# Router logits collected per tile inside the self-attention loop, and only the dense tiles turned behind it

## The reference

```python
logits = xt @ Wg                      # xt: layer norm of x, (4096, 128); Wg: (128, 8)
probs = softmax(logits)
_, top_idx = top_k(probs.T, 512)      # every expert takes its 512 best tokens
tok2exp = argmax over the experts that took the token, or over all if none did
out = sum_e gate_e * (gelu(xt @ W1[e]) @ W2[e])
```

## Time and profile before

| | before |
|---|---|
| median of 3 runs | 813.57 us (811.36 to 815.04) |
| the profiled execution | 814.61 us, span 812.5 us |
| PE busy | 698.5 us (86%) |
| DVE busy | 630.8 us (78%) |
| ACT busy | 510.2 us (63%) |
| POOL busy | 380.6 us (47%) |
| mean granted clock of PE | 0.935 |

### The profile page before, as it was taken

The page is one execution under the profiler, slowest core; times in us unless marked ns, Lnnn a source line. Parts: engine busy times, 40 slices in busy tenths (PEclk is TensorE's granted clock), DMA queues, the critical chain, the costliest instruction groups (busy, mean ns, idle before and its releaser), DMA issues.

```text
span 812.5 us, 27814 instructions
## 1 busy us (share of the span) xinstructions
PE 698.5 (86%) x9162; PEld 562.0 (69%) x9162; DVE 630.8 (78%) x1500; ACT 510.2 (63%) x1629; POOL 380.6 (47%) x380
## 2 busy tenths in 40 slices
PE   3572999999999999999999856799999689999565
PEld 1241767677777777777777645688888578889465
DVE  5462989899999999999999858589988656759721
ACT  1451777777777777787778624688888434545242
POOL 1250364456544654553544249477777320006365
PEclk9976999999999999999999979799999759999788
DMA  7558344444444444443440030000000000006980
GB/s 165 96 97 225 81 86 81 96 92 90 92 91 95 87 96 85 97 83 81 92 83 13 2 105 1 2 3 3 0 0 3 2 1 1 1 1 196 290 253 23
DMA packets 195179, 60.75 MB, mean 75 GB/s; under 512 B 147557, under 2 KB 193513, under 8 KB 195123
## 3 DMA queue, kind: packets, MB, share of 16 engines
q1 hardware_dynamic: 192000, 55.65, 30.7%
q0 software_dynamic: 1824, 3.96, 1.4%
q10 hardware_dynamic: 1298, 0.40, 0.2%
HBM read 51.58 MB, written 8.83 MB: 74 GB/s over the span
## 4 chain that ended last, share of the span: by engine, by line
PE 50%; SPq 17%; DVE 10%; issue 9%; ACT 7%; POOL 3%; ACTq 1%; DMA 1%; DVEq 0%; POOLq 0%
PE energy L485 22%; PE bank L485 15%; PE bank L488 13%; SPq L516 9%; ACT PR L644 6%; DVE STAT L1465 2%; SPq L522 2%; DVE X L1738 2%; SPq L566 1%; SPq L564 1%; POOL SX L907 1%; SPq L561 1%; POOL TQ L899 1%; ACTq L644 1%; SPq L539 1%
## 5 line engine op out<-in xcount | busy, mean ns | idle before, releaser
L644 ACT ACTIVATE PR<-energy,STAT 128x256 f32<-128x256 f32 x512 | 234.4, 482 | 107.5 <-DVE STAT L1465 107.5
L1465 DVE TENSOR_REDUCE STAT<-energy 128x512 f32 (+1 forms) x256 | 164.3, 685 | 27.2 <-PE energy L485 26.9
L488 PE MATMUL bank<-ident,PR 128*128 128x128 f32 x1024 | 152.5, 283 | 21.6 <-DVE PT L1482 16.8
L1482 DVE COPY PT<-bank 128x512 f32<-128x512 f32 x256 | 161.9, 672 | 1.3 <-PE bank L488 1.3
L488 PEld LDWEIGHTS bank<-ident,PR 128*128 128x128 f32 x1024 | 109.7, 142 | 52.6 <-issue 40.3
L833 POOL TENSOR_TENSOR QB<-QT,headmask 128x512 f32<-128x512 f32 x32 | 33.3, 1039 | 196.1 <-DMA MK<-in_mask_BxSxS_ik 122.1
L644 ACT ACTIVATION_READ_ACCUMULATOR PR<-energy,STAT (+1 forms) x512 | 110.1, 215 | 0.0
L840 POOL TENSOR_SCALAR MZ<-MK 128x512 bf16<-128x512 int32 x64 | 94.3, 1491 | 0.0
L485 PEld LDWEIGHTS bank<-wv_s,CT 128*128 128x128 f32 x512 | 68.7, 196 | 32.3 <-issue 31.8
L485 PE MATMUL bank<-CT,wk_s 128*128 128x512 f32 x128 | 68.5, 618 | 7.2 <-DVE CT L1489 7.2
L485 PE MATMUL bank<-PT,VT 128*32 128x128 f32 x2048 | 70.1, 278 | 0.2 <-DVE PT L1482 0.2
(11 more groups left out here) (268 smaller groups left out, 1340.6 us busy)
## 6 DMA issues: line engine op xcount, KB each, us to landing
CX<-in_ctx SPq DMA_DIRECT2D x512, 32.0 KB, 2.2
MK<-in_mask_BxSxS_ik SPq DMA_DIRECT2D x128, 128.0 KB
rows_in<-fill SPq DMA_DIRECT2D x1, 3483.0 KB, 19.0
X<-in_x SPq DMA_DIRECT2D x4, 512.0 KB, 7.7
VLT<-v_last SPq DMA_DIRECT2D x4, 512.0 KB, 8.2
QT<-in_L_ffn_W SPq DMA_DIRECT2D x16, 128.0 KB
OT<-in_L_ffn_W SPq DMA_DIRECT2D x16, 128.0 KB
PAY<-rows_in SPq DMA_DIRECT2D x2, 903.0 KB, 8.2
```

The lines of the kernel that those rows point to most:

```text
L488: return nc.tensor.transpose(o, i, ident[0:n, 0:n])
L644: nc.scalar.activation(PR[:, b, g, :], EB[:, g, e * KEYS:(e + 1) * KEYS], ACT.Exp, bias=STAT[:, bass.ds(t, 1), b, 1, g:g + 1].rearrange("p ...
L1465: V.tensor_reduce(STAT[:, bass.ds(t, 1), b:b + 2, 1, g:g + 1].rearrange("p a b g -> p (a b g)"), EB[:, g, :].rearrange("p (e k) -> p e k", ...
L1482: V.tensor_copy(PT[:, k % 2, e, 2 * half:2 * half + 2, :].rearrange("p g k -> p (g k)"), psum[1 if e else 7]).then_inc(ev_t, 1)
```

## The change

The logits are taken apart. With x2 = x1 + O @ w_o, mean m2 and r2 = 1/std2 of x2, and xn1 = (x1 - m1) / std1, the tile that self-attention has turned anyway:

logits = r2 * (std1 * (xn1 @ Wg) + O @ (w_o @ Wg) + (m1 - m2) * colsum(Wg)).

So inside self-attention PE multiplies two stationary tiles that it has there, xt and SO, by 8 columns each: xt with wg_s, and SO with wlog = sw_o @ wg_s, which is made once in the course of cross-attention. The results of all tiles stay in one PSUM bank (2 x 256 columns). Behind the loop DVE puts them together over 128x256. The statistics of the second norm get tiles of their own (mv2, std2, rstd2), since std and mean of the first are still needed. The normalisation of X moves to GpSimd: tiles 0 to 11, turned by PE in three groups (`turn_dense`) into banks 4 and 5 and copied by ACT behind the exponential; then the 20 others straight into PAY, with no transpose. router_step(0) stands between the second and the third group.

```diff
@@ ACT, in the loop of cross-attention's end
             for u in range(NT // 4 + 1):
+                if u == 4:
+                    act.wait_ge(lg_tr, 1)
+                    nc.scalar.activation(SO[:, 0, :], psum[4][:, 0:P], ACT.Copy).then_inc(lg_wo, 1)
+                if u == 6:
+                    act.wait_ge(lg_pe, 1)
+                    nc.scalar.activation(wlog[:, :], psum[5][:, 0:2 * E], ACT.Copy).then_inc(lg_w, 1)
@@ ACT, behind self-attention
             act.wait_ge(n2_std, 1)
-            nc.scalar.activation(std[:, :], std[:, :], ACT.Sqrt).then_inc(n2_rstd, 1)
-            def evac_router(u, h):
...
-            for u in range(NT // 4):
-                evac_router(u, u % 2)
+            nc.scalar.activation(std2[:, :], std2[:, :], ACT.Sqrt).then_inc(n2_rstd, 1)
+            nc.scalar.activation(warm[:, :], warm[:, :], ACT.Exp)
             act.wait_ge(t_act, 1)
             nc.scalar.activation(PRB[:, :, :], PRB[:, :, :], ACT.Exp).then_inc(t_exp, 1)
+            for u in range(LATE):
+                act.wait_ge(r_tr, u + 1)
+                wait_reuse(act, r_xl, u - 1)
+                nc.scalar.activation(xg[:, u % 2, :], psum[4 + u % 2], ACT.Copy).then_inc(r_xt, 1)
+                nc.scalar.activation(XH[:, u * 512:(u + 1) * 512], psum[4 + u % 2], ACT.Copy).then_inc(r_xh, 1)
@@ GpSimd, behind self-attention
-            for u in range(LATE):
-                input_rest(u, u % 2)
-            pool.wait_ge(a_x2, NT)
+            pool.wait_ge(r_inv, 1)
+            for u in range(LATE + 1):
+                if u < LATE:
+                    wait_reuse(pool, r_tr, u - 1)
+                    for j in range(4):
+                        normalised(xn[:, u % 2, j, :], 4 * u + j).then_inc(r_xn, 1)
+                if u:
+                    input_rest(u - 1, (u - 1) % 2)
+            for t in range(DENSE, NT):
+                normalised(PAY[:, t - DENSE, 0:P], t).then_inc(r_pn, 1)
             nc.gpsimd.tensor_copy(PAY[:, :, P:2 * P], X[:, DENSE:NT, :]).then_inc(pay_x, 1)
@@ PE, in the loop of cross-attention's end
+                if u == 3:
+                    pe.wait_ge(ld_s, N_S)
+                    pe.wait_ge(m_inv, 1)
+                    tr(psum[4][:, 0:P], sw_o[:, :]).then_inc(lg_tr, 1)
+                if u == 5:
+                    pe.wait_ge(lg_wo, 1)
+                    mm(psum[5][:, 0:E], SO[:, 0, :], wg_s[:, :])
+                    mm(psum[5][:, E:2 * E], ones_s, wg_s[:, :]).then_inc(lg_pe, 1)
@@ PE, in project(t, j) and project_out(t, j)
+                mm(psum[1][:, bass.ds(NT * E + t * E, E)], xt[:, j, :], wg_s[:, :])
+                mm(psum[1][:, bass.ds(t * E, E)], SO[:, j, :], wlog[:, 0:E])
                 mm(psum[7][:, P:2 * P], SO[:, j, :], sw_o[:, :]).then_inc(a_wo, 1)
@@ PE, behind self-attention
-            for u in range(NT // 4 + 1):
-                if u < NT // 4:
-                    turn_router(u, u % 2)
-                if u:
-                    logits(u - 1, (u - 1) % 2)
+            def turn_dense(u):
+                if u == 0:
+                    pe.wait_ge(a_sx, NT)
+                wait_reuse(pe, r_xt, u - 1)
+                wait_reuse(pe, r_xh, u - 1)
+                for j in range(4):
+                    pe.wait_ge(r_xn, 4 * u + (j + 1))
+                    last = tr(psum[4 + u % 2][:, j * P:(j + 1) * P], xn[:, u % 2, j, :])
+                last.then_inc(r_tr, 1)
...
+            def first_of_group(i):
+                pe.wait_ge(r_xl, i + 1)
+                if i == 0:
+                    pe.wait_ge(ld_ffn, 32)
+                    pe.wait_ge(w1_l, 1)
+                    pe.wait_ge(r_lg, 1)
...
+            turn_dense(0)
+            turn_dense(1)
             router_step(0)
+            turn_dense(2)
@@ DVE, behind self-attention
-            moments_to_rstd(n2_std, n2_rstd)
-            for u in range(NT // 4 + 2):
-                if u < NT // 4:
-                    norm_router(u, u % 2)
-                if u >= 2:
-                    keep_logits(u - 2, u % 2)
+            moments_to_rstd(n2_std, n2_rstd, mv=mv2, std=std2, split=True)
+            added, own = (psum[1][:, k * NT * E:(k + 1) * NT * E].rearrange("p (i e) -> p i e", e=E) for k in range(2))
+            dve.wait_ge(a_wo, NT)
+            link(V.tensor_tensor(rmx[:, :], mv[:, :, 0], mv2[:, :, 0], ALU.subtract))
+            link(V.tensor_tensor(PRB[:, :, :], own, over_experts(std[:, :]), ALU.mult))
+            V.tensor_tensor(PRB[:, :, :], PRB[:, :, :], added, ALU.add).then_inc(r_lg, 1)
+            dve.wait_ge(r_lg, 1)
+            link(V.tensor_tensor(KEY[:, :, :], over_experts(rmx[:, :]),
+                                 wlog[:, E:2 * E].rearrange("p (a e) -> p a e", a=1).broadcast_to([P, NT, E]), ALU.mult))
+            link(V.tensor_tensor(PRB[:, :, :], PRB[:, :, :], KEY[:, :, :], ALU.add))
+            dve.wait_ge(n2_rstd, 1)
+            V.reciprocal(rstd2[:, :], std2[:, :]).then_inc(r_inv, 1)
+            dve.wait_ge(r_inv, 1)
+            link(V.tensor_tensor(PRB[:, :, :], PRB[:, :, :], over_experts(rstd2[:, :]), ALU.mult))
```

More of the change, by code:

```diff
@@ L141, in perceiver_block @@
         shift = sb("shift", [P, NT])
+        mv2 = sb("mv2", [P, NT, 2])
+        std2 = sb("std2", [P, NT])
+        rstd2 = sb("rstd2", [P, NT])
+        wlog = sb("wlog", [P, 2 * 8])
         STAT = sb("STAT", [P, NT, BT, 2, NG])
@@ L404, in perceiver_block @@
         w1_l = sem("w1_l")
+        r_inv = sem("r_inv")
+        r_pn = sem("r_pn")
         r_lg = sem("r_lg")
-        r_cp = sem("r_cp")
+        lg_tr = sem("lg_tr")
+        lg_wo = sem("lg_wo")
+        lg_pe = sem("lg_pe")
+        lg_w = sem("lg_w")
         t_act = sem("t_act")
@@ L954, in input_rest, with normalised @@
                                         XH[:, bass.ds(u * 512, 512)], ALU.subtract).then_inc(r_xl, 1)
-            for u in range(LATE):
-                input_rest(u, u % 2)
-            pool.wait_ge(a_x2, NT)
+            def normalised(dst, t):
+                return nc.gpsimd.tensor_scalar(dst, X[:, t, :], mv2[:, t:t + 1, 0], rstd2[:, t:t + 1],
+                                               ALU.subtract, ALU.mult)
+            pool.wait_ge(r_inv, 1)
[8 more added lines that the diff above has]
+                normalised(PAY[:, t - DENSE, 0:P], t).then_inc(r_pn, 1)
             nc.gpsimd.tensor_copy(PAY[:, :, P:2 * P], X[:, DENSE:NT, :]).then_inc(pay_x, 1)
@@ L964, in _ @@
             pool.wait_ge(filled, 16)
-            pool.wait_ge(r_xn, NT)
+            pool.wait_ge(r_pn, SORTED)
             pool.wait_ge(s_gate, 1)
@@ L1158, in _ @@
                     out_project(u - 1, (u - 1) % 2)
+            pe.wait_ge(lg_w, 1)
             pe.wait_ge(wqk_ok, 1)
@@ L1221, in _ @@
                           (1, self_values), (4, turn_probs)], NT, 4, 6)
-            pe.wait_ge(a_x2, NT)
-            def turn_router(u, h):
+            def turn_dense(u):
+                if u == 0:
+                    pe.wait_ge(a_sx, NT)
                 wait_reuse(pe, r_xt, u - 1)
-                wait_reuse(pe, r_xh, min(u - 1, LATE))
+                wait_reuse(pe, r_xh, u - 1)
                 for j in range(4):
                     pe.wait_ge(r_xn, 4 * u + (j + 1))
-                    t = 4 * u + j
-                    last = tr(psum[h][:, j * P:(j + 1) * P], PAY[:, t - DENSE, 0:P] if t >= DENSE else xn[:, h, j, :])
+                    last = tr(psum[4 + u % 2][:, j * P:(j + 1) * P], xn[:, u % 2, j, :])
                 last.then_inc(r_tr, 1)
[L1235 to L1240, removed]
-            for u in range(NT // 4 + 1):
-                if u < NT // 4:
-                    turn_router(u, u % 2)
-                if u:
-                    logits(u - 1, (u - 1) % 2)
[L1249 to L1252, removed]
+            def first_of_group(i):
[4 more added lines that the diff above has]
+                    pe.wait_ge(r_lg, 1)
             def hidden(i, e, between):
                 u = i * E + e
+                if e == 0:
+                    first_of_group(i)
                 for j in range(FC):
@@ L1269, in expand @@
                 pe.wait_ge(f_g, u * FC + FC)
-                if not (isinstance(u, int) and u < 2):
+                if u < 2:
+                    pe.wait_ge(r_xh, LATE)
+                else:
                     pe.wait_ge(f_keep, u - 1)
@@ L1380, in link, with moments_to_rstd @@
                 dve.wait_ge(dve_c, chain[0])
-            def moments_to_rstd(st_sem, rs_sem, count=1, tiles=slice(0, NT), done=None):
+            def moments_to_rstd(st_sem, rs_sem, count=1, tiles=slice(0, NT), done=None, mv=mv, std=std, split=False):
                 me, mo = stats[:, tiles, 1], stats[:, tiles, 4]
@@ L1398, in moments_to_rstd @@
                 V.scalar_tensor_tensor(std[:, tiles], mv[:, tiles, 1], 0.25, std[:, tiles], ALU.mult, ALU.add).then_inc(st_sem, 1)
+                if split:
+                    return
                 dve.wait_ge(rs_sem, count)
```

16 lines of the change are left out of this document (removed).

## The result

| | before | after |
|---|---|---|
| median of 10 runs | 813.08 us (811.36 to 815.04) | 820.02 us (816.16 to 821.51) |
| the profiled execution | 814.61, span 812.5 | 821.51, span 819.5 |
| mean granted clock of PE | 0.935 | 0.932 |

The changed kernel is slower by 0.84%: ratio 1.0084, 95% interval 1.0070 to 1.0099. I had forecast 812.5 and a range of 806 to 819.5.

The account below looks back on a forecast made before the run. Bound: the chain of self-attention loop, router-logit stretch, dense experts with bisection, then sorted rows. Stretch -13.0, loop +7.7 and +1.0, port +3.0, cross-attention +0.2 sum to -1.1 us on 813.57: 812.5 us, range 806 to 819.5.

Parts of the forecast that it names:

- the loop's: Self-attention loop: two added products per tile cost +7.7 us, their register addresses +1.0 us.
- GpSimd's price for a normalisation: Between loop and experts: one 128x128 f32 normalisation on GpSimd takes 0.60 us, bounds 0.455 and 0.80.
- the stretch: From last residual to first expert matmul: transposes, logit products and DVE normalisations go, so experts start 13.0 us earlier.
- The port: During the experts: GpSimd work delays DVE's `trial` and `thr` in four bisection rounds, 2.6 us, plus 0.4 for the copy: +3.0.
- What bounds the loop: Self-attention loop: a chain through the engines every two tiles sets 7.40 us, while PE alone needs 3.40 a tile.
- PE's own step: Self-attention loop: PE's work per tile grows from 3.40 by 0.44 to 3.84 us; counting only this, 4.5 us in all.
- the two-tile loop: Self-attention: chain over PE, ACT, DVE and GpSimd once per two tiles grows from 7.40 to 7.84 us, 3.92 a tile.
- Cross-attention: One transpose, two products and two copies added where GpSimd sets the pace: +0.2 us (0 to 1).
- rival C: Slower: added weight loads in self-attention fall wholly on the path, 14.4 us plus 1.8 for registers; 820.0 us, chance 0.12.
- C's point of decision: Self-attention loop: the added cost per tile from which this slower case decides, 0.28 us.
- B's loop: Faster: self-attention grows only by PE's own step, 4.5 us, registers and port cost nothing; 805.3 us, chance 0.30.
- D's condition: Slower: a GpSimd normalisation costs 1.0 us, delaying experts and meeting seven bisection rounds (+6.3); 820.6 us, chance 0.10.

Follow-up runs that it names:

- experiments 6: Kernel before the change, plus both products per tile at fixed addresses, placed at the end of PE's step behind turn_probs: ratio 1.0053 to before, loop 136.3 us.
- experiment 8: Changed kernel with both products moved to the end of PE's step, behind turn_probs: ratio 0.9982 to before, median 810.72 us.
- the second execution: The unaltered changed kernel profiled again later, beside other runs: ratio 1.0081 to before, loop 142.8 us.
- experiment 7: Changed kernel with the PAY copy on ACT, dense tiles normalised on DVE and router steps two `between` calls later: ratio 0.9951 to before, median 808.67 us.
- experiment 3: Changed kernel without the two products per tile in the self-attention loop: ratio 0.9911 to before, median 805.22 us.

## Why the prediction was wrong

**The steps that failed.** The parts that I had added up to -1.1 us came to +3.7 in the profiled execution (+1.8 in the second), and the medians moved by +6.9. The term that was off most is the loop's: 7.7 and 1.0 us for the two products, where it grew by 11.6 (10.9). Next is GpSimd's price for a normalisation: 0.60 us, where it took 0.79 to 0.83, so that the stretch shrank by 11.8 and not 13.0. The port's 3.0 us was near in size but came from another instruction than the one that I priced. And the first stage, for which I had no term, took longer in every kernel with the change. Each in turn:

**What bounds the loop: right.** PE's own step of 3.40 + 0.44 and the two-tile loop of 7.40 + 0.44 were both confirmed, the first by the 3.84 of experiments 6 and 8, the second by the 3.95 a tile of the written-out steps (3.92 forecast) and by what happens when the products leave it. One reading behind it was luck: I took the step from 581.62 to 585.02 for one without a wait, but the QD ahead of it ended at 584.95 (583.91 + 1.04), 0.07 us before the scores, the distance of the steps that wait. That PE's own step is 3.40 is borne out only by 3.84 - 0.44. What I didn't do is draw the conclusion that stood in my own sum: it had 4.5 us for the products if only PE's own step counts, and the loop with the products at the end grew by 4.4.

**Size of the loop's term: too small.** Forecast +8.7, measured +11.6 (10.9 the second time). Over 26 tiles in the steady part 4.02 - 3.70 = 0.32 a tile, 8.3 us, where I had 0.22 and 1.0 for the registers, 6.7. From the start of the scores to the start of turn_probs, and from there to the scores two steps on, it is 3.01 + 4.38 in most steps of before, 3.23 + 4.38 with one product, 3.53 + 4.38 with two at fixed addresses, and 3.65 + 4.43 with two at register addresses. So the two products put 0.52 us into the two-tile loop, where I had 0.44 (and where the same two add 0.44 to PE's own step), and the register addresses another 0.17. The rest, 3.3 us, is filling and draining, for which 2.0 stood. About 1 us of it is the distance between the first two scores alone: 4.10 in after and 3.19 in the second execution, against 2.96 before; among the kernels with both products it was 3.2 to 4.5, so that part varies by about a microsecond.

**The stretch: right in kind, 1.2 us short.** -11.8 for -13.0. The term that was mis-sized is the normalisation on GpSimd. The groups of after:

```profile
L968 POOL TENSOR_SCALAR PAY<-X,mv,rstd 128x128 f32<-128x128 f32 x20 | 15.6, 794 | 0.0
L968 POOL TENSOR_SCALAR xn<-X,mv,rstd 128x128 f32<-128x128 f32 x12 | 9.9, 833 | 9.0 <-DVE rstd L1673 9.0
```

It takes 0.79 alone, where I took 0.60 near the row of the same operation and size that writes bf16; my upper bound was 0.80. Twelve make 12 x 0.19 = 2.3 us more. The meetings with DVE, for which I added 1.3, made it 0.83 instead of 0.79, 0.5 in all. The Trainium skill (GPSIMD Engine Reference, section 3.1), by which I had estimated a shorter instruction and a start a microsecond earlier, erred on the same side; the measurement decides.

**The port: right in sum (+3.0, measured +4.0 and 2.8), wrong in its cause.** I gave 2.6 us to four rounds of `trial` and `thr` beside normalisations and 0.4 to the copy. In after the operations beside normalisations have a mean of 0.22, 0.18 and 0.18 us for `trial`, `trial_next` and `thr`, against 0.16 each once GpSimd is silent: together 0.1 us a round, not 0.75; the longest was 0.28, and the rounds were 2.7 us long, not 3.3. The copy did nearly all of it, in a single instruction: with the copy on ACT the stage was back at 62.6. That could have been read from the trace of before. There the same copy lay beside DVE's normalisations: four took 1.83 us without it, and 3.67 with it.

```profile
649.85 1.83 DVE L1406 TENSOR_SCALAR PAY<-X,mv,rstd 128x128 f32<-128x128 f32 x4
...
652.30 3.67 DVE L1406 TENSOR_SCALAR PAY<-X,mv,rstd 128x128 f32<-128x128 f32 x4
653.06 2.32 POOL L960 COPY PAY<-X 128x2560 f32<-128x2560 f32 x1
```

I had looked for long GpSimd instructions where they stood and not asked which of them the change moves beside the bisection. The Trainium skill (SBUF — State Buffer, "Who interferes with whom") says of such a meeting that the blocked engine waits for the whole instruction of the other; the copy and the subtractions of experiment 7 agree, the normalisations, 0.79 us each, don't. In after the rows don't show the copy first either: `thr` begins at 690.04, 0.26 us ahead of it and during the last normalisation, and still ends with the copy. What decides there is open. PE's idle time can cost more than itself: in after and in experiment 8 PE's weight loads stood still for 2.55 and 2.54 us, its clock then fell to 0.50, and the stage took 66.5 us. In the second execution and in experiment 3 they stood for 2.00 and 1.90 us, the clock stayed at 1.00, and the stage took 65.3. Of the 1.2 us between the two pairs some 0.6 is the longer idle time itself; the other 0.6 goes with the clock, by this estimate, and not the whole of what a stall costs beyond its length.

**Cross-attention: nothing** (34.4 against 34.5), as forecast within 0.2.

**What stays open.** The stages that I looked at sum up to +3.7 us in one profiled execution and +1.8 in the other, the medians differ by 6.9. By the profiled executions the rest lies in the first and the last stage. Profiled executions of kernels with the change had a first stage of 475.4 to 478.8 (seven, mean 477.1), those without 471.8 to 476.7 (five, mean 474.1). The granted clock of PE between 40 and 80 us was anything from 0.71 to 0.78 with the change and from 0.71 to 0.79 without, so a part may be chance. A part isn't likely to be: the longest wait of the first stage is DVE's for a tile of the context, with PE idle behind it, here in before and in after:

```profile
76.53 0.71 DVE L1489 STREAM_TRANSPOSE CT<-CX 128x512 f32<-128x512 f32 x1 [16.74 <-DMA CX<-in_ctx]
```

```profile
79.57 0.71 DVE L1517 STREAM_TRANSPOSE CT<-CX 128x512 f32<-128x512 f32 x1 [18.68 <-DMA CX<-in_ctx]
```

It was 16.7 to 17.3 us in the five profiled executions without the change (mean 16.9) and 18.0 to 18.7 in the seven with it (mean 18.2). So the changed kernel has 1.3 us of its own there, in a place whose code it didn't touch. Why, and what makes up the other 1.7 us between the means, no run settles.

**The rivals.** The measured median is the number of rival C, by chance: C had 16.2 us for the loop, which took 11.6, and the difference was made up by other terms. C's point of decision, 0.28 us a tile, was passed (11.6 / 32 = 0.36). Its mechanism was only half true: not every added weight load falls on the path, but a loop of two tiles in which both stand. B's loop (4.5) is what experiments 6 and 8 show, for products that stand elsewhere. D's condition (1.0 us a normalisation) didn't come about, but the 0.66 from which I had called the kernel slower was passed (0.83 in the stretch); its meetings in the bisection's rounds weren't seen.

## What to carry to other kernels

An addition to a loop has two prices: one to the engine's own step, and one to every chain through other engines in which its place in the order puts it. Compute both, then put it behind the last instruction that another engine waits for; here that place made 0.9982 of 1.0081. When a change moves work, list what each other queue now has beside the tightest loop, and look up in the trace what the longest single instruction of these did to its neighbours: here one copy of 2.32 us held up the bisection more than twenty normalisations of 0.79 us did.

## What the runs showed of the hardware

- An f32 product of a full 128x128 weight tile with 8 columns takes 0.22 us of PE at the upper clock (one adds 0.22 to the time from scores to turn_probs, two at the end of the step 0.44 to it; two at their first place added 0.52).
- Writing to an address from a register costs PE some 0.04 us a product (1.3 us for 32 in the loop, of one profiled execution each) where it stands on the path.
- A wait of PE of 0.1 to 0.3 us ahead of a matmul may not show as idle: with 19.93 of 20 us busy the step still shortened by 0.2 us (4.04 to 3.85) when the products were moved. What tells it is the distance from the end of the operand's writer to the start of the reader, 0.07 to 0.13 where it waits and 0.37 where it doesn't.
- A tensor_scalar with two scalars from a tile (128x128, f32) takes 0.79 us on GpSimd and 3.17 / 12 = 0.26 on DVE.
- One GpSimd copy of 2.32 us held a DVE instruction of one integer a partition for 2.4 us (one of three integers for 2.0 in the second execution); twenty GpSimd instructions of 0.79 us lengthened DVE's small two-input operations by 0.02 to 0.06 us on the mean.
